# Perceiver kernel, expert phase of layer 0: token weights by small TensorE products of transposed key factors, kept in DRAM; expert products in split rounded form

## Chip, cores and metric

One core of one Trainium2 chip runs the whole program. The metric is the device time of one execution in microseconds (us); the time of a version is the median over its runs. Lower is better.

## What is computed

A two-layer model on 1024 tokens (32 x 32) of width 512. Layer 0 is cross attention, gated attention with an MLP, and a feed-forward block with a routed part; layer 1 is cross attention over 257 context rows, a scan and a last MLP. The change lies in the feed-forward block of layer 0:

```
q = (x @ Wq) per head h of 4;  sim = q @ keys          # 64 first keys x, 64 second keys y
top 8 of each, all 8 x 8 sums, top 8 of those           # expert number x * 64 + y, 2048 experts
w = silu(x @ down_embed[idx]) * softmax(scores)
experts = sum over heads and 8 choices of w * up_embed[idx]
mlp = silu(x @ Wg + bg) * (x @ Wu + bu) @ Wd + bd
return mlp + experts
```

The kernel does not gather experts. For every token it makes a dense row of 2048 token weights (the softmax weight of each chosen expert, zero elsewhere, summed over the four heads), and computes silu(down @ y) times the token weights, times up. Weights of choices with a first key of 32 or more all go to the last expert.

## The kernel before

Every engine has its own program, and semaphores tie them. Stages end with a drain of all engines. Tokens are columns; C2 = 2 chunks c of 512 tokens, TT = 8 tiles t of 128 tokens, o numbers blocks of 128 outputs, and the hidden width of 2048 is done in NQ = 4 quarters j of 512. PSUM has eight banks of 128x512: four (`open_act`) are emptied by ACT, four (`open_dve`) by DVE, each in the order in which TensorE opens them.

Products of the MLP are in *split rounded form* (`split_linear`, L739): each fp32 operand is the sum of a rounded part (fp32r, "high") and a rest ("low"), and high\*high + low\*high + high\*low takes 12 matmuls of 128x512 for one unit of 512 inputs, 128 outputs, 512 tokens. ACT makes the high parts, DVE the low parts, of the weights too (`piece_high`, `piece_low`, eight pieces ahead). Products in plain fp32 (`linear`, L498) take 4 matmuls a unit.

Stage C, in the order of its steps:
- Layer norm, queries (`cq`), similarities (`sim`, L787), and the split of the normed input y (`y_high`, `y_low`).
- Gated MLP. For each quarter j: eight pairs of units `cg` (gate, emptied by ACT with Silu, L1418) and `cu` (up, emptied by DVE, L2046), then eight units `cd` (`down`, L749), which wait for the low part of the hidden tile (`hidden_low`, L2035, waited for at L751). Between these, DVE routes the token tiles, two per quarter, piece by piece, in the list `ROUTE` (L1998): `route_keys` (top 8), `route_pairs`, `route_chosen`, `route_counts` (how many second keys go with each first key), `route_ranks` (the rank of each second key, L1973), `route_factors`.
- Expert phase. 32 steps n = (quarter j, tile t). `factors_in` and `factors_out` are the expert products in plain fp32 on y and on the weighted hidden tile. The token weights of a step: `products` on ACT makes 32 copies of 64 columns, each scaled by one factor (L1397); `spread` on DVE (L2004 to L2024) compares 2048 elements, multiplies, adds the heads; `factor_rows` (L820) transposes on TensorE; `weigh` (L2026) multiplies into the hidden tile.

Small products on parts of the array stand in other stages: `scores` (L664, 32x32 tiles) and `values` (L678, four tiles on the diagonal) in the attention of stage B, `weighted` (L953, four column tiles) in stage D.

Stage D begins with layer norm and `memory(0, ...)` (L857), products of context and the weights `wmh`, `wml`.

SP issues all DMAs in one written order; `load(i)` brings one weight block of 1 MB and first waits until its slot's last user is done.

```
STEPS, LEAD, LAG = TT * NQ, 3, 5
...
v.tensor_tensor(tmp, RC["Tx"][:, t, :, xs].unsqueeze(3).to_broadcast([128, PH, 8, 64]),
                RC["Ry"][:, t].unsqueeze(2).to_broadcast([128, PH, 8, 64]), ALU.is_gt)
```

Of the kernel before, what the change touches and what calls it, by code (L numbers as in the profile page):

```python
# [35 lines left out]
def constant_tables():  # L36
# [24 lines left out]
    tabs["rank"] = np.tile(np.arange(8.0) - 8.0, (128, 1))  # L61
# [34 lines left out]
def perceiver(nc, dram, out):  # L96
# [6 lines left out]
    with ctx:  # L103
# [56 lines left out]
        with ExitStack() as until_last:  # L160
# [5 lines left out]
            wmh = shared_r("wmh", [128, 2, 4, 512])  # L166
# [3 lines left out]
            wml = shared_r("wml", [128, 2, 4, 512])  # L170
# [28 lines left out]
        with ExitStack() as until_last:  # L199
# [4 lines left out]
            rank_eq, count_eq = small_ints("rank_eq", [128, 256, 8]), small_ints("count_eq", [128, 128, 8])  # L204
            iota8, rank8 = small_ints("iota8", [128, 64, 8]), small_ints("rank8", [128, 1, 8])
            keys8, counts8 = small_ints("keys8", [128, 2 * PH, 8]), small_ints("counts8", [128, PH, 8])
        rank_eq, count_eq, iota8, rank8, keys8, counts8 = (x[:, :, :] for x in (rank_eq, count_eq, iota8, rank8, keys8, counts8))
# [5 lines left out]
        def region(spec, base=R, limit=RN):  # L213
# [18 lines left out]
        slot_full = [sem(f"slot_full{i}") for i in range(6)]  # L232
        spilled = [sem(f"spilled{i}") for i in range(2)]
# [17 lines left out]
            "a_khi", "a_qhi", "a_whi", "a_wlo", "a_chi", "a_clo", "a_bhi", "a_blo", "a_ahi", "a_ctx", "c_topin", "c_topexp", "c_p", "c_kb", "c_fac", "c_ee", "c_mul", "c_y", "c_wq",  # L251
# [69 lines left out]
        expert_slots = iter([(turn[0] + i) % 2 for i in range(2)] + [2, 3, 4, 5] + [(turn[0] + i) % 2 for i in range(2)])  # L321
        for j in range(-1, NQ + 1):
            if j + 1 < NQ:
                plan(("ce", j + 1), rows4("downT", 0, 512 * j + 512), next(expert_slots))
            if j >= 1:
                plan(("cf", j - 1), rows4("L0_ffn_up_embed", 512 * j - 512), next(expert_slots))
        D_FIRST = len(loads)
        for h in range(2):
            plan(("dm", h), rows4("L1_xattn_Wm", 0, 512 * h), 4 + h)
# [23 lines left out]
        def first_high_of(i):  # L353
# [6 lines left out]
        RC = region([("sim", (8, 512)), ("kb", (4, 128)), ("Tx", (8, PH, 32)), ("Ex", (8, PH, 32)), ("Ry", (8, PH, 64)),  # L360
                     ("Ey", (8, PH, 64)), ("eq", (1, 2048)), ("s", (4, 512)), ("xv", (1, 8)),
                     ("pj", (2, 512)), ("tv", (8, 8)), ("ti", (8, 8)), ("cand", (PH, 64)), ("rep", (PH, 64)),
                     ("t8", (PH, 8)), ("na", (PH, 8)), ("z", (1, 4)), ("rz", (1, 4)), ("ge", (PH, 8)), ("rs", (PH, 8)),
                     ("sd", (8, 64)), ("sel", (PH, 64))])
# [3 lines left out]
        SJ = [H[:, 0], H[:, 1], XN]  # L368
# [14 lines left out]
        EE = [RC["sim"][:, 0:4].rearrange("p t n -> p (t n)"), RC["sim"][:, 4:8].rearrange("p t n -> p (t n)"),  # L383
              RC["s"].rearrange("p t n -> p (t n)")]
        ct = H[:, 0, 0:2, :].rearrange("p k (b m) -> p (k b m)", b=2).rearrange("p (k b m) -> p k b m", k=4, b=2)
        ct_first = arena[:, 3, :, :].rearrange("p k (b m) -> p k b m", b=2)
# [58 lines left out]
        def b1_order(j):  # L445

            return [(o, c) for c in range(C2) for o in range(4)] if j == 0 else [(o, c) for o in range(4) for c in range(C2)]
# [14 lines left out]
        def _(pe):  # L462
# [286 lines left out]
            def down(name, j, ready, first):  # L749
                for c in range(C2):  # L750
                    pe.wait_ge(ready, first + 8 * j + (4 * c + 4 if (name, j) == ("b2", 0) else 7 + c))  # L751
                    for o in range(4):
                        b = open_dve((name, j, c, o))
                        split_linear(b, (name, j), o, hid_high, hid_low, c).then_inc(dve_bank_full, 1)
                        if c == C2 - 1:
                            piece_used[piece_no[((name, j), o)]] = (dve_bank_full, UV.n)


            for j in range(NQ):
                for o, c in b1_order(j):  # L760
# [14 lines left out]
            pe.wait_ge(S["c_wq"], 16)  # L775
            for c in range(C2):
                features(2, c)
                normed(pe, 2, c)
# [27 lines left out]
            def factors_in(n):  # L806
                j, t = n // TT, n % TT
                if t == 0:
                    weight(("ce", j))
# [347 lines left out]
        def _(act):  # L1157
# [286 lines left out]
            for t in range(4):  # L1444
                hidden(0, t)
# [1138 lines left out]
```

## Time and profile before

| | |
|---|---|
| median of 3 runs | 2295.05 us (2292.68 to 2303.32) |
| the profiled execution | 2294.39 us, its span 2292.6 us |
| mean granted TensorE clock | 0.971 |
| busy in the span | PE 2114.7, DVE 1280.5, ACT 917.4, POOL 94.8 us |
| first gated-MLP matmul of stage C | starts at 720.3 us |
| first expert matmul | starts at 988.9 us |
| last expert matmul | ends at 1256.1 us |

The profiled execution's own time is 1.8 us more than its span. "Busy" of TensorE counts overlapped matmuls once; a matmul of 128x512 in fp32r shows 389 ns but the next begins 227 ns after it. "Granted clock" is TensorE's clock as a share of 2.4 GHz; a half is the level of 1.2 GHz. A name like L746 is a line of the kernel before.

### The profile page before, as it was taken

Reading aid. Unit: us, or ns where it says so; the run is one execution under the profiler, and the core shown is the slowest. Engines: PE = TensorE matmul, PEld = TensorE weight load, DVE = VectorE, ACT = ScalarE, POOL = GpSimd, SP = SyncE. Lnnn points to the kernel's source line nnn. Section 1 sums busy time; section 2 is a strip of 40 time slices with the busy share of each in tenths; the row PEclk is TensorE's granted clock in tenths of the full one; section 3 lists DMA queues with packets and bytes.
Section 4 is the critical chain, followed back from the end, with each engine's and each line's share of the span. In section 5 each row is a group of like instructions: output and inputs, shape, how many; then the busy total and the mean of one; then the engine's idle time right before and its main releaser. Section 6 shows DMA issues by size and latency. Waiting matters only on the chain. (4 is left out here: it accounts for less than half of the span.)

```text
span 2292.6 us, 35473 instructions
## 1 busy us (share of the span) xinstructions
PE 2114.7 (92%) x14758; PEld 1530.3 (67%) x14758; DVE 1280.5 (56%) x2082; ACT 917.4 (40%) x2208; POOL 94.8 (4%) x119
## 2 busy tenths in 40 slices
PE   6989888689999999989998999999999999988899
PEld 5763444368876888844445788777878778774587
DVE  4246388463343887799998310445344443536563
ACT  3224333142334333489997332322232322313342
POOL 0000001000000000100000000100000000000122
PEclk9999899789999999999999999999999999999999
DMA  6120000111210101120002144412121121232000
GB/s 236 42 77 0 1 2 2 39 37 56 72 44 1 56 19 56 56 92 1 19 0 94 36 142 133 134 43 84 42 84 43 52 74 42 66 111 90 1 1 37
DMA packets 84871, 127.06 MB, mean 55 GB/s; under 512 B 6998, under 2 KB 48470, under 8 KB 84248
## 3 DMA queue, kind: packets, MB, share of 16 engines
q1 hardware_dynamic: 84712, 124.79, 16.4%
q8 instruction: 118, 1.93, 0.4%
q14 instruction: 41, 0.34, 0.1%
HBM read 109.83 MB, written 14.94 MB: 54 GB/s over the span
## 5 line engine op out<-in xcount | busy, mean ns | idle before, releaser
L1167 ACT ACTIVATE R<-bank 128x512 f32<-128x512 f32 (+3 forms) x157 | 93.0, 598 | 460.9 <-PE bank L866 332.3
L1397 ACT ACTIVATE R<-R 128x64 f32<-128x64 f32 x1024 | 248.3, 366 | 0.0
L866 PE MATMUL bank<-cth,wmh 128*128 128x512 f32 x512 | 209.6, 409 | 12.4 <-ACT arena L1494 6.3
L866 PE MATMUL bank<-cth,wml 128*128 128x512 f32 x512 | 203.7, 398 | 0.0
L866 PE MATMUL bank<-ctl,wmh 128*128 128x512 f32 x512 | 203.5, 397 | 0.0
L501 PE MATMUL bank<-XN,arena 128*128 128x512 f32 x320 | 144.9, 606 | 0.4 <-ACT R L1328 0.4
L866 PEld LDWEIGHTS bank<-cth,wmh 128*128 128x128 f32 x512 | 97.2, 190 | 41.9 <-issue 22.3
L501 PE MATMUL bank<-Y,arena 128*128 128x512 f32 x256 | 117.3, 604 | 0.0
L2119 DVE COPY Y<-bank 128x512 f32<-128x512 f32 x128 | 79.2, 682 | 59.3 <-PE bank L904 59.3
L866 PEld LDWEIGHTS bank<-cth,wml 128*128 128x128 f32 x512 | 97.1, 190 | 22.6
L501 PEld LDWEIGHTS bank<-XN,arena 128*128 128x128 f32 x320 | 60.9, 195 | 75.5 <-issue 73.4
L866 PEld LDWEIGHTS bank<-ctl,wmh 128*128 128x128 f32 x512 | 97.3, 190 | 20.4
L746 PE MATMUL bank<-hid_high,piece_high 128*128 128x512 f32 x256 | 100.0, 391 | 6.2 <-DVE hid_low L2037 6.2
L1494 ACT ACTIVATE arena<-bank,small 128x289 f32<-128x289 f32 x128 | 62.6, 503 | 100.3 <-PE bank L915 53.5
L746 PE MATMUL bank<-y_high,piece_high 128*128 128x512 f32 x256 | 99.7, 389 | 0.0
L746 PE MATMUL bank<-hid_low,piece_high 128*128 128x512 f32 x256 | 99.6, 389 | 0.0
L746 PE MATMUL bank<-hid_high,piece_low 128*128 128x512 f32 x256 | 99.6, 389 | 0.0
L746 PE MATMUL bank<-y_high,piece_low 128*128 128x512 f32 x256 | 99.6, 389 | 0.0
L746 PE MATMUL bank<-y_low,piece_high 128*128 128x512 f32 x256 | 99.6, 389 | 0.0
L2106 DVE TENSOR_TENSOR ctl<-H,cth 128x2048 fp32r<-128x2048 f32 x15 | 34.4, 2292 | 103.4 <-ACT cth L1469 103.4
L1205 ACT ACTIVATE piece_high<-arena 128x512 fp32r<-128x512 f32 x80 | 48.8, 624 | 104.5 <-PE bank L746 103.4
L501 PEld LDWEIGHTS bank<-Y,arena 128*128 128x128 f32 x256 | 49.5, 195 | 60.1 <-issue 59.8
(412 smaller groups left out, 4464.7 us busy)
## 6 DMA issues: line engine op xcount, KB each, us to landing
H<-in_ctxT SPq DMA_DIRECT2D x30, 512.0 KB, 5.1
arena<-in_L_attn_mlp_w SPq DMA_DIRECT2D x8, 1024.0 KB, 5.4
arena<-spill SPq DMA_DIRECT2D x32, 256.0 KB, 5.5
spill<-R SPq DMA_DIRECT2D x3, 2048.0 KB, 8.3
spill<-XN SPq DMA_DIRECT2D x3, 2048.0 KB, 8.3
arena<-in_L_ffn_Wg SPq DMA_DIRECT2D x4, 1024.0 KB, 6.8
arena<-in_L_ffn_Wu SPq DMA_DIRECT2D x4, 1024.0 KB, 5.2
arena<-in_L_ffn_Wd SPq DMA_DIRECT2D x4, 1024.0 KB, 5.4
```

What stands on the lines that cost most here:

```text
L501: last = mm(bank, w[:, k, cols_], x[:, k, xc], start=(k == 0), stop=(k == 3 and not more))
L746: last = mm(b[:, :], w_, x_[:, k, ch(c)], start=(k == 0 and i == 0), stop=(k == 3 and i == 2))
L866: last = mm(b[:, :].rearrange("p (a c) -> p a c", a=2), w_, c_[:, k, :, :], start=(k == 0 and n_ == 0), stop=(k == 3 and n_ == 2))
L1167: fn(dst, src, ACT.Copy).then_inc(act_bank_free, 1)
L1205: fn(piece_high[:, n % PIECES], W(name)[:, :, tl(o)], ACT.Copy).then_inc(S["w_high"], 1)
L1397: last = fn(EE[n % 3][:, a:a + 64], RC["Ey"][:, t, h, :], ACT.Copy, scale=RC["Ex"][:, t, h, 8 * j + x:8 * j + x + 1])
L1494: fn(RDa["p"][:, g, 320 * (bb % 2):320 * (bb % 2) + 289], b[:, 0:289], ACT.Exp, bias=small[:, 16 + x:17 + x], scale=HD1 ** -0.5, accum_out ...
L2106: v.tensor_tensor(ctl[:, :, :, :], ct if pr else ct_first, cth[:, :, :, :].bitcast(f32), ALU.subtract).then_inc(S["d_clo"], 1)
L2119: v.tensor_copy(RD["vt"][:, 2 * (bb % 2) + blk, 512 * half:512 * half + 512], b[:, :]).then_inc(dve_bank_free, 1)
```

## The change

The 32 steps of the expert phase are gone, with `products`, `spread`, `factor_rows`, `weigh` and `route_ranks`, and the addition on POOL that put y together again.

Token weights are now made in the gated MLP, one token tile at a time. For each head and rank b of a second key, `route_first_keys` makes 32 numbers over the first keys, `route_second_keys` makes a 0/1 row over the 64 second keys, and DVE transposes both in 32x32 blocks, so that (head, b) lies on 32 partitions. `expert_sums(t, half)` then makes, for each of 64 tokens of a half, two products of 32 rows by 64 by 16 on TensorE, 128 in all, and two more for the last expert; ACT empties the banks (`sums_of`), SP stores a tile of 1 MB to DRAM and later reads it back in 256 KB blocks.

The expert phase is then like the MLP: `ce` and `cf` are units of 12 matmuls in split rounded form; DVE multiplies the token weights in. The order of queries and similarities changes, the first tile is routed before the MLP, and the first weights and contexts of stage D are loaded and split earlier.

TensorE, from the diff:

```diff
+                        elif o in half_after:
+                            expert_sums(2 * j + 1, half_after.index(o))
+
+            def expert_sums(t, half):
+
+                pe.wait_ge(S["c_pairs"], t + 1)
+                two = {i: open_act(("w", t, i)) for i in (2 * half, 2 * half + 1)}
+                for r in range(32):
+                    for par in range(2):
+                        for i, b in two.items():
+                            heads = slice(32 * i, 32 * i + 32)
+                            mm(b[64 * par:64 * par + 64, 16 * r:16 * r + 16], RC["yT"][heads, :, r], RC["xT"][heads, par:32:2, r],
+                               start=(r == 0), stop=False, tile_position=(32 * i, 64 * par), skip_group_check=True)
+                for i, b in two.items():
+                    mm(b[:, :].rearrange("p (r m) -> p m r", m=16)[:, 15, :], RC["xv"][:, 0, :], tab("ident")[:, 32 * i:32 * i + 32],
+                       start=False, stop=True, skip_group_check=True).then_inc(act_bank_full, 1)
 
...
-            pe.wait_ge(S["x_low"], 2 * C2)
+            similarities(1)
             for j in range(NQ):
                 for o in range(4):
                     for c in range(C2):
+                        if j == 0 and o == 0:
+                            pe.wait_ge(S["x_low"], C2 + c + 1)
                         b = open_act(("cg", j, o, c))
                         split_linear(b, ("cg", j), o, y_high, y_low, c).then_inc(act_bank_full, 1)
                         b = open_dve(("cu", j, o, c))
                         split_linear(b, ("cu", j), o, y_high, y_low, c).then_inc(dve_bank_full, 1)
-                    piece_used[piece_no[(("cg", j), o)]] = (act_bank_full, UA.n)
+                        if 2 * o + c in (1, 2):
+                            expert_sums(2 * j, 2 * o + c - 1)
+                    piece_used[piece_no[(("cg", j), o)]] = (act_bank_full, UA.at[("cg", j, o, C2 - 1)] + 1)
                     piece_used[piece_no[(("cu", j), o)]] = (dve_bank_full, UV.n)
-                down("cd", j, S["h_low"], 32)
...
-            def factor_rows(n):
-                j, t = n // TT, n % TT
-                pe.wait_ge(S["c_p"], n + 1)
-                b = open_dve(("pt", j, t))
-                for e in range(4):
-                    last = nc.tensor.transpose(b[:, tl(e)], RC["pj"][:, t % 2, tl(e)], tab("ident"))
-                last.then_inc(dve_bank_full, 1)
...
+                down("cd", j, S["h_low"], 32, (1, 2))
+
+            for j in range(NQ):
+                for o, c in up_order(j):
+                    b = open_act(("ce", j, o, c))
+                    split_linear(b, ("ce", j), o, y_high, y_low, c).then_inc(act_bank_full, 1)
+                    if c == C2 - 1:
+                        piece_used[piece_no[(("ce", j), o)]] = (act_bank_full, UA.n)
+                down("cf", j, S["h_low"], 64)
```

ACT and DVE:

```diff
+            def sums_of(t, half):
+
+                if t and half == 0:
+                    act.wait_ge(sums_out, 16 * t)
+                for i in (2 * half, 2 * half + 1):
+                    copy_out(RC["sums"][:, :, 32 * i:32 * i + 32], unit(("w", t, i))[:, :].rearrange("p (r m) -> p m r", m=16))
...
+            for j in range(NQ):
+                for i, (o, c) in enumerate(up_order(j)):
+                    u = 8 * j + i
+                    activated(("ce", j, o, c), 32 + u)
+                    if i:
+                        act.wait_ge(S["c_scaled"], u)
+                        hidden_high(32 + u - 1, *up_order(j)[i - 1])
+                    if c == C2 - 1:
+                        split_high(piece_no[(("ce", j), o)] + PIECES)
+                act.wait_ge(S["c_scaled"], 8 * j + 8)
+                hidden_high(32 + 8 * j + 7, *up_order(j)[7])
...
-                on_act(("ce", j, 3 if t < 4 else 7))
-                b = unit(("pt", j, t))
-                x = SJ[j % 3][:, :, tl(t)]
-                v.tensor_tensor(x, b[:, :].rearrange("p (e n) -> p e n", e=4), x, ALU.mult).then_inc(dve_bank_free, 1)
-
-            def hidden_low(u):
-                j, o, c = u // 8, u // 2 % 4, u % 2
+                v.tensor_reduce(RC["xv"][:, 0, 127:128], RT["rs"].rearrange("p h a -> p (h a)"), AX.X, ALU.add)
+                step(v.tensor_tensor(RC["Ex"], RT["sd"][:, 0, 0:128].rearrange("p (h x) -> p h x", h=PH), rz.to_broadcast([128, PH, 32]),
+                                     ALU.mult))
+
+            first_keys = RC["xf"].rearrange("p (h b) x -> p h b x", h=PH)
+
+            def route_first_keys(t):
+
+                for b in range(8):
+                    last = v.scalar_tensor_tensor(first_keys[:, :, b, :], RC["Tx"], float(b), RC["Ex"], ALU.is_gt, ALU.mult)
+                step(last)
+                step(v.tensor_tensor(RC["xf"], RC["xf"], RT["sd"][:, 0, 128:160].unsqueeze(2).to_broadcast([128, 32, 32]), ALU.mult))
+                v.transpose(RC["xT"], RC["xf"].rearrange("p n x -> p x n"))
+
+            def route_second_keys(t):
+
+                step(v.tensor_tensor(RC["yf"], iota8.unsqueeze(1).to_broadcast([128, PH, 64, 8]),
+                                     keys8[:, 4:8, :].unsqueeze(2).to_broadcast([128, PH, 64, 8]), ALU.is_equal))
+                v.transpose(RC["yT"].rearrange("p y (h b) -> p y h b", h=PH), RC["yf"].rearrange("p h y b -> p y h b")
+                            ).then_inc(S["c_pairs"], 1)
+
+            ROUTE = [route_keys, route_pairs, route_chosen, route_counts, route_factors, route_first_keys, route_second_keys]
+            DOWN_PIECES = {(0, 0): 1, (0, 1): 2, (0, 2): 3, (0, 3): 4, (1, 0): 5, (1, 1): 6}
+
```

SP:

```diff
+            sums = dram["sums"]
+
+            def store_sums(t):
+                sp.wait_ge(act_bank_free, UA.at[("w", t, 3)] + 1)
+                sp.dma_start(sums[:, :, tl(t)].rearrange("m p n -> p m n"), RC["sums"]).then_inc(sums_out, 16)
+
+            def load_sums_of(u):
+                j, (o, c) = u // 8, up_order(u // 8)[u % 8]
+                if u >= 8:
+                    sp.wait_ge(S["c_scaled"], u - 7)
+                else:
+                    sp.wait_ge(S["c_pairs"], u + 1)
+                sp.wait_ge(sums_out, 16 * (4 * c + 4))
+                sp.dma_start(RC["sim"][:, u % 8, :], sums[4 * j + o, :, ch(c)]).then_inc(sums_in[u % 8], 16)
+
+            load(first_split + 2)
...
+                store_sums(2 * j)
+                load(first_split + 3 * j + 4)
+                store_sums(2 * j + 1)
+                load(first_split + 3 * j + 5)
+                if j < NQ - 1:
+                    load(first_split + 3 * j + 6)
+            for u in range(4):
+                load_sums_of(u)
+            load(first_split + 15)
+            for u in range(4, 8):
+                load_sums_of(u)
+            for h in range(2):
+                sp.dma_start(dm_raw[:, h], rows4("L1_xattn_Wm", 0, 512 * h)).then_inc(S["d_dm"], 16)
+            for u in range(8, 32):
+                load_sums_of(u)
+                if u in (15, 23):
+                    load(first_split + 16 + (u // 8 - 1) * 2)
+                    load(first_split + 17 + (u // 8 - 1) * 2)
 
             two = dram["ctxT"].rearrange("(k p) (b m) -> p k b m", p=128, m=M)
 
```

On TensorE in the first quarter of the gated MLP, as it stands now (L764 and L767 are `expert_sums`, L742 is `split_linear`; R holds the transposed factors), rows just ahead of the first half of tile 0's small products and behind it:

```order
L742 MATMUL bank<-y_high,piece_high 128x512
L742 MATMUL bank<-y_low,piece_high 128x512
L742 MATMUL bank<-y_high,piece_low 128x512
L764 MATMUL bank<-R 64x16 x128
L767 MATMUL bank<-consts,R 128x32 x2
L742 MATMUL bank<-y_high,piece_high 128x512
L742 MATMUL bank<-y_low,piece_high 128x512
```

Such a group of 130 stands at 16 places of the gated MLP, four in each quarter; before, there was none, and L746 followed on L746.

On DVE before, at the fifth and the sixth pair of units of the first quarter (L1976 and L1978 are `route_ranks`, L1960 to L1996 `route_factors`):

```order
L2037 TENSOR_TENSOR hid_low<-R,hid_high 128x512
L1976 TENSOR_TENSOR rank_eq<-iota,keys 128x2048
L1978 TENSOR_TENSOR rank_eq<-rank_eq,rank 128x2048
L2046 SCALAR_TENSOR_TENSOR R<-bank,cols,R 128x512
L2037 TENSOR_TENSOR hid_low<-R,hid_high 128x512
L1960 TENSOR_TENSOR rank_eq<-rank_eq 128x256x4
L1960 TENSOR_TENSOR rank_eq<-rank_eq 128x256x2
L1983 TENSOR_TENSOR R<-rank_eq 128x256
```

On DVE now, ahead of the first `cu` unit (L2005), the end of tile 0's routing (L1969 to L1972 are `route_first_keys`, L1976 and L1978 `route_second_keys`):

```order
L1961 TENSOR_TENSOR R<-R 128x128
L1969 SCALAR_TENSOR_TENSOR R<-R 128x4x32 x8
L1971 TENSOR_TENSOR R<-R 128x1024
L1972 STREAM_TRANSPOSE R<-R 128x1024
L1976 TENSOR_TENSOR R<-iota,keys 128x2048
L1978 STREAM_TRANSPOSE R<-R 128x2048
L2005 SCALAR_TENSOR_TENSOR R<-bank,cols,R 128x512
L1898 MAX R<-R 128x8 x8
```

The rank products of the list are gone; the two new pieces stand behind the sixth and the seventh `cu` unit of each quarter, and for tile 0 ahead of the first.

## Rows read from the trace of the kernel before

**Rows 1.** Windows: us, busy (x instructions) of PE, PEld, DVE, ACT, POOL; clock, DMA, GB/s.
```profile
720.00:785.00 65.00, 63.46 (x282) 52.30 (x282) 47.02 (x145) 23.33 (x36) 0.00 (x0) 1.00 0.05 17
1030.00:1230.00 200.00, 185.92 (x495) 82.80 (x495) 189.89 (x155) 200.00 (x815) 0.00 (x0) 1.00 0.07 24
```

**Rows 2.** Timeline of PE: start, us, what [idle before]; 38 matmuls lie from 980.03 to 988.64.
```profile
966.98 0.50 PE L746 MATMUL bank<-hid_high,piece_high 128*128 128x512 f32 x1 [1.54 <-DVE hid_low L2037]
...
980.03 0.39 PE L746 MATMUL bank<-hid_high,piece_high 128*128 128x512 f32 x1
988.64 0.39 PE L746 MATMUL bank<-hid_high,piece_low 128*128 128x512 f32 x1
988.87 13.89 PE L501 MATMUL bank<-Y,arena 128*128 128x512 f32 x32
...
1245.13 10.96 PE L501 MATMUL bank<-H,arena 128*128 128x128 f32 x96
```

**Rows 3.** Groups of small and large products: xcount, busy, mean ns, idle before.
```profile
L664 PE MATMUL bank<-H 32*32 32x32 f32 x1024 | 11.7, 214 | 8.4 <-issue 8.4
L678 PE MATMUL bank<-R 32*32 32x33 f32 x1024 | 15.9, 237 | 24.1 <-DVE R L1831 15.1 <-issue 8.9
L953 PE MATMUL bank<-Y,R 128*32 128x64 f32 x2048 | 35.4, 221 | 2.5 <-DVE XN L2181 1.5 <-issue 1.1
L664 PEld LDWEIGHTS bank<-H 32*32 32x32 f32 x1024 | 10.8, 112 | 9.9 <-issue 9.1 <-DVE H L1851 0.2
L746 PEld LDWEIGHTS bank<-y_high,piece_high 128*128 128x128 f32 x256 | 48.1, 188 | 9.9
```

**Rows 4.** Timeline of PE, one set of 256 small products, and what follows.
```profile
268.27 1.74 PE L664 MATMUL bank<-H 32*32 32x32 f32 x161
272.31 1.14 PE L664 MATMUL bank<-H 32*32 32x32 f32 x95 [2.30 <-issue]
273.87 6.43 PE L501 MATMUL bank<-XN,arena 128*128 128x512 f32 x8 [0.42 <-ACT R L1328]
```

**Rows 5.** Groups of DVE in the gated MLP; last, two of other stages.
```profile
L2046 DVE SCALAR_TENSOR_TENSOR R<-bank,cols,R 128x512 f32<-128x512 f32 x32 | 24.0, 750 | 37.2 <-PE bank L746 37.2
L2037 DVE TENSOR_TENSOR hid_low<-R,hid_high 128x512 fp32r<-128x512 f32 x32 | 21.8, 682 | 0.4
L1927 DVE MAX8 R<-R 128x8 f32<-128x64 f32 x64 | 8.8, 210 | 0.0
L1983 DVE TENSOR_TENSOR R<-rank_eq 128x256 f32<-128x256 bf16 x8 | 4.9, 617 | 0.3
L1985 DVE TENSOR_TENSOR R<-R 128x256 f32<-128x256 f32 x8 | 3.3, 418 | 0.0
L1996 DVE TENSOR_TENSOR R<-R 128x128 f32<-128x128 f32 x7 | 2.0, 284 | 0.0
L1769 DVE STREAM_TRANSPOSE R<-R 128x1024 f32<-128x1024 f32 x1 | 1.2, 1245 | 6.6 <-DMA R<-scratch 6.6
1239.31 2.29 DVE L2015 TENSOR_TENSOR R<-R 128x2048 f32<-128x2048 f32 x1
```

**Rows 6.** Timeline of ACT ahead of the gated MLP.
```profile
720.58 0.60 ACT L1167 ACTIVATE R<-bank 128x512 f32<-128x512 f32 x1 [0.30 <-PE bank L787]
721.19 1.28 ACT L1418 ACT_TABLE_LOAD   x1
```

**Rows 7.** Timeline of PE, after longer idle times.
```profile
1012.91 0.83 PE L820 MATMUL bank<-consts,R 128*128 128x128 f32 x4 [2.41 <-DVE R L2021]
1013.54 5.16 PE L501 MATMUL bank<-Y,arena 128*128 128x512 f32 x8
...
1273.69 0.77 PE L866 MATMUL bank<-cth,wmh 128*128 128x512 f32 x1 [3.16 <-DVE R L1671]
```

**Rows 8.** Page, DMA issues: out<-in xcount, KB each, us to landing.
```profile
arena<-spill SPq DMA_DIRECT2D x32, 256.0 KB, 5.5
spill<-R SPq DMA_DIRECT2D x3, 2048.0 KB, 8.3
```

More of the change, by code:

```diff
@@ L232, in perceiver @@
         slot_full = [sem(f"slot_full{i}") for i in range(6)]
+        sums_in = [sem(f"sums_in{i}") for i in range(8)]
+        sums_out = sem("sums_out")
         spilled = [sem(f"spilled{i}") for i in range(2)]
@@ L775, in _, with similarities @@
             pe.wait_ge(S["c_wq"], 16)
+            def similarities(c):
+                on_act(("cq", 3, c))
+                pe.wait_ge(S["c_kb"], 16)
+                for t in range(4 * c, 4 * c + 4):
+                    b = open_act(("sim", t))
+                    for j in range(4):
+                        last = mm(b[:, tl(j)], H[:, 0, j, tl(t)], RC["kb"][:, j, :], start=True, stop=True)
+                    last.then_inc(act_bank_full, 1)
             for c in range(C2):
                 features(2, c)
+                if c:
+                    similarities(0)
                 normed(pe, 2, c)
@@ L1033, in _ @@
                 released[(w, half)] = (S["d_plo"], 4 * (g_ + 1))
-            for h in range(2):
-                released[("dm", h)] = (stage_done, 4 * (stage[0] + 1))
             end_stage()
@@ L1371, in _, with similarities @@
             end_stage()
+            def similarities(c):
+                for t in range(4 * c, 4 * c + 4):
+                    copy_out(RC["sim"][:, t, :], unit(("sim", t))[:, :])
             warm()
@@ L1433, in _ @@
+                sums_of(2 * j + 1, 0)
+                sums_of(2 * j + 1, 1)
                 for o in range(4):
                     split_high(piece_no[(("cd", j), o)] + PIECES)
-            def hidden(j, t):
-                b = unit(("ce", j, t))
-                fn(SJ[j % 3][:, t % 4, ch(t // 4)], b[:, :], ACT.Silu).then_inc(act_bank_free, 1)
-            products(1)
-            act.wait_ge(S["h_low"], 32 + 8 * NQ)
-            products(2)
-            act.wait_ge(dve_bank_full, UV.at[("cd", 3, C2 - 1, 3)] + 1)
@@ new lines, in _ @@
+            inputs_low(0)
+            inputs_low(1)
+            for piece in ROUTE[4:]:
+                piece(0)
+            for j in range(NQ):
+                for i in range(8):
+                    o, c, u = i // 2, i % 2, 8 * j + i
+                    on_act(("cg", j, o, c))
+                    b = unit(("cu", j, o, c))
+                    v.scalar_tensor_tensor(RC["s"][:, u % 4, :], b[:, :], col("L0_ffn_bu", 4 * j + o), RC["s"][:, u % 4, :],
+                                           ALU.add, ALU.mult).then_inc(dve_bank_free, 1)
+                    if i:
+                        hidden_low(u - 1, (i - 1) // 2, (i - 1) % 2)
+                    if i < 7:
+                        ROUTE[i](2 * j + 1)
+                    elif j < NQ - 1:
+                        route_keys(2 * j + 2)
+                    if c == C2 - 1 and o < 3:
```

375 lines of the change are left out of this document (121 added, 254 removed).

## The prediction

> **What bounds the kernel now.** I read the windows first, then TensorE's timeline, then the groups of instructions. In the gated MLP TensorE is busy 63.46 of 65 us, ACT 23.33 and DVE 47.02 at the full clock, so this stretch costs what its matmuls cost [rows 1]. In the expert phase ACT is busy all of 200 us, DVE 189.89 and TensorE 185.92 [rows 1]: three engines are near full, and ACT, with the scaled copies of `products`, has no gap at all. The timeline gives the two prices of a large product [rows 2]. In split form 38 steps take from 980.03 to 988.64 us, 0.227 us each, so a unit of 12 costs 2.72 us. The plain fp32 ones (32 in 13.89 us) cost 0.434 us, 1.74 us a unit. The split form is dearer for TensorE; what it buys is an expert phase in which nothing else is needed. The phase lasts from 988.9 to 1256.1 us, 267.2 us [rows 2].
>
> **What goes.** All 267.2 us. With them go 1024 copies on ACT, the comparing and adding on DVE and 128 transposes; they lie beside each other within that time, so they aren't counted again.
>
> **Expert products.** 4 quarters x 16 units x 2.72 us = 174.1 us on TensorE. Beside it a unit of `ce` asks of DVE a scaling, a low part and a weight's low part, at 0.68 us each [rows 5]: 2.0 us of 2.72. ACT has three passes of about 0.6 us [rows 6]. So TensorE bounds it. At the turn to `cf` it waits: before, the turn in the MLP cost 1.54 us for a product on DVE and a low part [rows 2]; now the last unit passes Silu, the scaling and the low part of the one before, some 0.69 + 0.68 + 0.68 and hops, 2.25 us. The first quarter walks its chunks so that it needs no wait, so 3 x 2.25 = 6.8 us. Together 180.9 us.
>
> **Small products.** 2048 of 32 rows by 64 weight columns by 16 columns, none like them in the trace. Three groups are near [rows 3]: 32x32x32 in sixteen tiles, busy 11.7 us for 1024, 11 ns each; 32x32x33 on four tiles in turn, 15.5 ns; 128x32x64 on four column tiles, 17.3 ns. Ours alternate among four tiles. A weight load takes 112 ns for 32 columns and 188 for 128 [rows 3], 0.8 ns a column, so ours carries more load and less product. Lower bound: 11 ns. Upper bound: a load of 64 columns that nothing hides, 64 x 0.8 = 51 ns plus a part of the product, 55 ns. I take 17 ns, by the two groups on four tiles. A group of 130 is then 2.2 us, 0.24 for the two full-height products and 0.2 for the change of tiling (estimates), 2.6 us; sixteen make **42 us**. The fetch gap of 2.30 us came after 161 products in a row [rows 4]; a group of 130 between large products should stay below it, so I charge none.
>
> A rule speaks against this price. The rows hold products of 32 columns at 11 ns. The Trainium skill, "TensorEngine Tiling (Array Packing)", section Performance Considerations, says that each matmul carries some 60 cycles of overhead, whatever its few columns: 25 ns at 2.4 GHz. By it 2048 would cost 51 us, and the sum would come out 16 us higher, at no change; the rows are faster than the rule, and they decide.
>
> **DVE's list.** Ranks go (two passes over 2048 bf16, then sums); in come eight products over 128 numbers, one over 1024, a transpose of 1024, a comparison of 2048 into fp32 and a transpose of 2048. A pass over 64 numbers is issued every 0.14 us, one over 128 lasts 0.28 [rows 5], so eight take about 1.6; 1024 take 1.2 (0.28 for 128, 2.29 for 2048). The transpose of 1024 took 1.245 us with neighbours in a row, but now reads numbers 128 bytes apart. A sum that reads every 16 bytes took 617 ns for 256 results, an ordinary one 418 [rows 5]; with that ratio, 1.9. So `route_first_keys` costs 4.7 us, `route_second_keys` 2.3 + 2.4 = 4.7. They stand behind the sixth and seventh `cu`. There DVE has the scaling, a low part, the piece and two weights' low parts, 0.75 + 0.68 + 4.7 + 1.37 = 7.5, and then 0.75 + 0.68 + 4.7 = 6.1 us, against 2 x 5.44 of TensorE: it is 2.7 us behind when the last `cu` is done, and `cd` waits for `hidden_low` behind that. Four quarters: **10.8 us** over the 1.54 that each turn has now. In the `cd` stretch DVE needs about 28 us for TensorE's 21.8 and two groups; it makes that up before the next sums are asked for, nothing charged. Bounds for this term: 0 if passes overlap more, 20 if both transposes are read at the strided price.
>
> **The first tile.** It must be routed before the second `cu`. Its first four pieces lie under the query products. `route_factors` needs ACT's exponentials, which come after the last similarity copies (ending 721.2 [rows 6], about 1 us later with the new order) and a table load of 1.28 us: 724.2. Then DVE has the rest of `route_factors` (nine small passes of 0.19 to 0.42 us, 2.3 in all) and the two new pieces, 2.3 + 4.7 + 4.7 us, to 736. TensorE, started at 720.3 as now (similarities and queries are only exchanged), gets there at 731.2. **4.8 us**, once.
>
> **The clock.** After an idle 2.41 us the next eight plain matmuls took 5.16 us in place of 3.60; after 3.16 us a split one shows 0.77 where 0.39 is usual [rows 7, 2]: the level of 1.2 GHz for some 3.5 us. After 1.54 us nearly nothing is lost [rows 2]. The change makes five waits of 4 us and more, at 2.1 us lost each, and three of 2.25, at 1.2: **14 us**; bounds 0 and 20.
>
> **At nothing.** ACT's 32 emptyings of token weights (0.6 us each, 19 us) lie in an MLP where it is a third busy [rows 1]; uncovered, a bank would come free late. SP's eight stores of 1 MB and 32 loads of 256 KB: 2 MB took 8.3 us to land and 256 KB 5.5 [rows 8]. A store is due a whole half quarter before its buffer is wanted; the loads of the second chunk need tile 7, stored some 20 us before. Each waits in SP's one queue behind weight loads that come two blocks early; if a load were late, Silu's buffer would hold TensorE after eight units, 21.8 us. POOL's addition was under TensorE. In stage D one wait (context split) goes and one (`memory_low`, 2.3 us behind the other low part) comes in its place; +-2.
>
> **Sum.** -267.2 + 180.9 + 42 + 4.8 + 10.8 + 14 = -14.7 us. Against the profiled execution (2294.4; span 2292.6 and 1.8 around it) that is 2279.7. The median shown is 0.7 above this execution, which I leave. **Forecast 2280 us.** Break-even is at a small product of 24 ns.
>
> **Rivals.**
> 1. *Weight loads aren't hidden (slower).* Place: each of the 16 groups. Two of every four small products load the same 32 partitions, and each load is as wide as two of the loads in the rows; columns lie 128 bytes apart, moving ones 256. On DVE such reading cost 1.5 times [rows 5]; nothing in the trace shows it for TensorE. For: 51 ns by slope. Against: 128x32 loads follow at 17.3 ns though 27 ns wide by the same slope, so they overlap. At 45 ns a product: 28 x 2048 = +57 us, **2337 us**. It decides from 24 ns on. The rule that points here is the Trainium skill's "SBUF — State Buffer", on 16-byte cachelines: full bandwidth wants two hits in a line. DVE's rows agree with it.
> 2. *Everything overlaps.* 11 ns a product, no clock lost: -13 - 14, **2253 us**. For: the sixteen-tile group. Against: fewer tiles here.
> 3. *The clock falls after each group.* After a set of 256 with its gap, eight plain matmuls took 6.43 us in place of 3.60 [rows 4]. Sixteen times 2.8: +45, **2325 us**. Against: the 128x32 products are spread over a stretch at full clock.
> 4. *Token weights come late from DRAM*, so that what went from ACT returns as a wait: one load time and a half at the start of the phase, +8, **2288 us**.
>
> **Chances.** Forecast 0.45 (its own range 2265 to 2296), rival 1 0.25, rival 2 0.15, rival 3 0.08, rival 4 0.07. A measurement of this kernel tells about 0.5%, 11.5 us, from no change. Faster by more: most of the forecast (0.29), rival 2 and a little of 4: 0.46. Slower by more: rivals 1 and 3 and a tail of the forecast: 0.36. Within: 0.18. The range of 8 in 10 reaches from rival 2 to the middle of rival 1: 2252 to 2338.
>
> **What would show it.** L764 in groups of 128 lasting 2.2 us: right; 5 us or more: rival 1. Large matmuls at 0.227 us right behind a group: rival 3 wrong. From the first `ce` to the last `cf` 181 us plus the clock's share; waits for `hidden_low` of 4.2 us four times, for `c_pairs` once. I am wrong if `ce` waits for the loads of sums, or if DVE comes so late that groups wait in every quarter.

## The result, and the profile after

The changed kernel takes 2426.8 us (median of 4 runs, 2419.0 to 2427.88) against 2295.39 us before (4 runs): 1.0566 times, 95% interval 1.0545 to 1.0588. The forecast was 2280 us with a range up to 2338, so the time lies outside the range and on the other side. The profiled execution has a span of 2425.1 us against 2292.6 of before, 132.5 us more.

The page's slices first. This is the granted clock in 40 equal slices, before and then now. In the second half it was near full before; now it sags over eight slices in a row, the gated MLP:

```profile
PEclk9999899789999999999999999999999999999999
PEclk9999888899998887878799999999999999999999
```

The groups of instructions for the small products, TensorE's matmuls and weight loads (PEld):

```profile
L764 PE MATMUL bank<-R 32*64 32x16 f32 x4096 | 139.0, 284 | 4.0 <-DVE R L1978 4.0
L764 PEld LDWEIGHTS bank<-R 32*64 32x64 f32 x4096 | 137.3, 224 | 10.0 <-issue 5.6 <-DVE R L1978 4.4
L767 PE MATMUL bank<-consts,R 128*128 128x32 f32 x64 | 17.0, 406 | 0.0
```

The program issues 2048 small products; the trace has 4096 records at L764. So **a float32 product is two records**, and all that I had priced by a row of the trace before was priced by the record. Busy 139.0 us over 4096 is 33.9 ns a record, 68 ns a product, where I had put 17.

The timeline of TensorE, the first two groups with what follows them (start, us, what, idle before):

```profile
737.18 8.62 PE L764 MATMUL bank<-R 32*64 32x16 f32 x256 [3.95 <-DVE R L1978]
745.73 1.06 PE L767 MATMUL bank<-consts,R 128*128 128x32 f32 x4
746.61 0.78 PE L742 MATMUL bank<-y_high,piece_high 128*128 128x512 f32 x1
747.18 0.63 PE L742 MATMUL bank<-y_low,piece_high 128*128 128x512 f32 x1
747.61 0.63 PE L742 MATMUL bank<-y_high,piece_low 128*128 128x512 f32 x1
...
753.76 8.65 PE L764 MATMUL bank<-R 32*64 32x16 f32 x256
762.34 1.06 PE L767 MATMUL bank<-consts,R 128*128 128x32 f32 x4
...
796.29 0.50 PE L742 MATMUL bank<-hid_high,piece_high 128*128 128x512 f32 x1 [3.88 <-DVE hid_low L1991]
```

A group lasts 8.6 us where I had 2.2, and seven or eight large matmuls behind it start 0.43 us apart in place of 0.227. Windows of the first group, then of the second group and of what follows it (length, busy with instructions of PE, PEld, DVE, ACT and POOL, then the clock):

```profile
737.20:741.00 3.80, 3.80 (x118) 3.80 (x119) 3.73 (x26) 0.64 (x1) 0.00 (x0) 0.50 0.00 0
741.00:745.70 4.70, 4.70 (x146) 4.70 (x144) 2.76 (x16) 0.00 (x0) 0.00 (x0) 0.50 0.03 7
753.80:758.00 4.20, 4.20 (x131) 4.20 (x132) 2.83 (x8) 0.00 (x0) 0.00 (x0) 0.84 0.02 4
758.00:762.30 4.30, 4.30 (x134) 4.30 (x132) 0.00 (x0) 0.00 (x0) 0.00 (x0) 0.50 0.01 4
762.50:764.50 2.00, 2.00 (x7) 1.81 (x8) 0.00 (x0) 1.08 (x2) 0.00 (x0) 0.50 0.00 0
```

Two things are to be seen. The clock falls from 2.4 to 1.2 GHz inside the second group, although TensorE has no gap, and stays low behind it; the first group, behind a wait of 3.95 us, runs at 1.2 GHz from its start. And the small products don't care: 256 records take 8.62 us in the first group and 8.65 in the second, of which a part ran at full clock, 33.7 and 33.8 ns each. What limits them isn't TensorE's clock.

The parts of the change, against the forecast's sum:

| part | forecast, us | measured, us | from |
|---|---|---|---|
| old expert phase gone | -267.2 | -267.2 | [rows 2] |
| expert products with their waits | 180.9 | 182.8 | timeline, 1201.86 to 1384.7 |
| small products, L764 and L767 | 42 | 156 | groups, 139.0 + 17.0 |
| first tile | 4.8 | 4.0 | timeline, 3.95 |
| four turns to `cd` | 10.8 | 9.3 | 4 waits of 3.88 for 1.54 |
| clock, large matmuls of the gated MLP | 14 | 42 | rest, below |
| before and behind (start of MLP, stage D) | 0 | 5.6 | 1.7 + 3.9 |
| sum | -14.7 | 132.5 | |

The gated MLP lasts from 722.0 to 1201.86 us, 479.9. Its large matmuls took 262.4 before (268.6 less four waits of 1.54). With 156 for the groups and 19.5 for five waits, 42 are left: what the large matmuls took longer at the lower clock. The forecast's 14 also held 3.6 for the turns of the expert phase; what these lost is in the 182.8. Of the 147 us between forecast and measurement 114 lie in the small products and 28 in the clock.

The 5.6 us before and behind can't be put down to the change: over the eleven profiled kernels with the new expert phase, this one and those of the experiments, the stretch ahead of the gated MLP takes 717.2 to 723.1 us and the one behind the expert phase 1036.7 to 1041.9, though the edits leave nearly all of the work there as it is.

### The profile page after: what moved, and what is told of

Same layout as the page of the kernel before. It is cut to its first block and busy times, and to the rows that moved or that the text cites. A ratio compares the mean times of both kernels' runs of the same rounds, so it can differ in the third digit from the quotient of the medians.

```text
span 2425.1 us, 43019 instructions
## 1 busy us (share of the span) xinstructions
PE 2252.5 (93%) x18950; PEld 1744.1 (72%) x18950; DVE 1153.6 (48%) x2066; ACT 725.1 (30%) x1279; POOL 83.7 (3%) x111
## 5 line engine op out<-in xcount | busy, mean ns | idle before, releaser
L1139 ACT ACTIVATE R<-bank 128x512 f32<-128x512 f32 x189 | 110.5, 597 | 632.0 <-PE bank L839 329.3
L742 PE MATMUL bank<-hid_high,piece_high 128*128 128x512 f32 x384 | 162.7, 424 | 21.6 <-DVE hid_low L1991 21.6
L742 PE MATMUL bank<-hid_low,piece_high 128*128 128x512 f32 x384 | 160.0, 417 | 0.0
L742 PE MATMUL bank<-hid_high,piece_low 128*128 128x512 f32 x384 | 159.0, 414 | 0.0
L742 PE MATMUL bank<-y_high,piece_high 128*128 128x512 f32 x384 | 158.2, 412 | 0.4 <-DVE y_low L1986 0.4
L742 PE MATMUL bank<-y_low,piece_high 128*128 128x512 f32 x384 | 156.2, 407 | 0.0
L742 PE MATMUL bank<-y_high,piece_low 128*128 128x512 f32 x384 | 155.5, 405 | 0.0
L764 PEld LDWEIGHTS bank<-R 32*64 32x64 f32 x4096 | 137.3, 224 | 10.0 <-issue 5.6
L764 PE MATMUL bank<-R 32*64 32x16 f32 x4096 | 139.0, 284 | 4.0 <-DVE R L1978 4.0
L839 PEld LDWEIGHTS bank<-cth,wmh 128*128 128x128 f32 x512 | 97.2, 190 | 42.0 <-issue 19.5
L742 PEld LDWEIGHTS bank<-hid_high,piece_high 128*128 128x128 f32 x384 | 79.3, 207 | 41.3 <-DVE hid_low L1991 24.5
```

The source lines that it names most:

```text
L742: last = mm(b[:, :], w_, x_[:, k, ch(c)], start=(k == 0 and i == 0), stop=(k == 3 and i == 2))
L764: mm(b[64 * par:64 * par + 64, 16 * r:16 * r + 16], RC["yT"][heads, :, r], RC["xT"][heads, par:32:2, r], start=(r == 0), stop=False, tile_ ...
L839: last = mm(b[:, :].rearrange("p (a c) -> p a c", a=2), w_, c_[:, k, :, :], start=(k == 0 and n_ == 0), stop=(k == 3 and n_ == 2))
L1139: fn(dst, src, ACT.Copy).then_inc(act_bank_free, 1)
```

## The experiments

Each edit is made to the changed kernel (2426.8 us) and timed beside the kernel before. Medians are given, and a ratio is to the kernel before, which came to 2293.6 to 2296.1 us beside them. Times without a ratio are of a single execution. Where a length of the gated MLP is given, it is read from the profiled executions (479.9 us in the change).

**Without the small products.**

```diff
-                for r in range(32):
+                for r in range(0):
...
-                       start=False, stop=True, skip_group_check=True).then_inc(act_bank_full, 1)
+                       start=True, stop=True, skip_group_check=True).then_inc(act_bank_full, 1)
```

The last pair lets the product of L767 open its bank, since nothing is written there before it.

> The changed kernel without the 2048 small products (32 rows by 64 by 16); the two full-height products of each group, the copies, the stores and loads and all of DVE's list stay. The token weights are therefore zero apart from the last expert's. Theory A (the groups of small products and the clock behind them are the whole loss): the gated MLP falls from 479.9 to about 268.6 + 13 of waits + 17 for the full-height products and their slow neighbours, some 300 us, and the time is near 2427 - 180 = 2247 us, below the kernel before. Rival B (DVE's longer list, the DRAM round trip or the new expert phase share the loss): above 2290 us.

2248.24 us, ratio 0.979 (0.9767 to 0.9812). All the rest of the change is a gain of 46 us. The gated MLP falls from 479.9 to 301.5 us, so the whole difference lies there. The groups cost 178.6 us: 139.0 at L764, 8.0 at L767 (17.0 before the edit, 9.0 now, mean 264 ns in place of 406), and 31.6, the rest, in the large matmuls behind them. That is the price of a small product, the place of rival 1, and rival 3 together.

**The layout.** Three kernels read the same number of bytes from other places, so that the token weights are wrong: neighbouring words on both sides, on the weight side alone, and on the moving side alone.

```diff
-  RC["yT"][heads, :, r]
+  RC["yT"].rearrange("p y t -> p (y t)")[heads, 64 * r:64 * r + 64]
-  RC["xT"][heads, par:32:2, r]
+  RC["xT"].rearrange("p x t -> p (x t)")[heads, 32 * r + 16 * par:32 * r + 16 * par + 16]
```

> The changed kernel, but the small products read 64 and 16 adjacent numbers of the same two tiles, in place of columns 128 and 256 bytes apart (the token weights are wrong numbers for that). Theory S (reading with a stride sets the 33.7 ns per record): 17 ns or less per record, a group under 5 us, time about 2427 - 16 x 4.3 = 2358 us or lower. Rival L (a load of 64 columns that nothing hides): unchanged, 33 ns and 2427 us. Rival C (the low clock sets it): unchanged too.

> Only the weight side (64 columns) reads adjacent numbers. If the stride counts and the load is the longer part: nearly all of the gain of the run with both sides packed. If the stride of the moving side counts: little.

> Only the moving side (16 columns) reads adjacent numbers. If the load of weights sets the pace: within 10 us of the changed kernel's 2427 us, 33 ns a record.

2363.45, 2364.09 and 2416.21 us; the gated MLP is 58, 56 and 11 us shorter. The first is 5 us above what was expected of it, the last just past the 10 us that it was given. The groups of each, in this order:

```profile
L764 PE MATMUL bank<-R 32*64 32x16 f32 x4096 | 75.1, 215 | 17.4 <-issue 13.5 <-DVE R L1978 4.0
```

```profile
L764 PE MATMUL bank<-R 32*64 32x16 f32 x4096 | 76.8, 217 | 16.7 <-issue 12.8 <-DVE R L1978 4.0
```

```profile
L764 PE MATMUL bank<-R 32*64 32x16 f32 x4096 | 125.5, 270 | 4.0 <-DVE R L1978 4.0
```

The weight side alone, whose columns lie 128 bytes apart in the change, takes 62 us off the busy time and both sides 64; the moving side alone takes off 13.5, and 2 beside a packed weight side. Packed, a record comes to about 16 ns at full clock: in the timeline of the first of these kernels 227 of them take 3.55 us, 15.6 ns, and behind them comes an idle time that nothing in the trace releases. The first group, at 1.2 GHz from its start to its end, needs 7.03 us for its 256, 27.5 ns each, so a packed record does depend on the clock:

```profile
732.34 7.03 PE L764 MATMUL bank<-R 32*64 32x16 f32 x256 [3.97 <-DVE R L1978]
747.79 3.55 PE L764 MATMUL bank<-R 32*64 32x16 f32 x227
752.35 1.04 PE L764 MATMUL bank<-R 32*64 32x16 f32 x29 [1.00 <-issue]
...
900.87 3.92 PE L764 MATMUL bank<-R 32*64 32x16 f32 x256
```

It looks like the gap of [rows 4], which I had ruled out for groups of 130; with two records a product the groups are of 256. It gives back 13 of the 62 to 64 us. In the changed kernel, at 34 ns a record, it doesn't show, so it didn't cost anything there.

**Packed, with the right numbers.** VectorE's transpose writes token by token, so its writes are strided in TensorE's place.

```diff
-  v.transpose(RC["yT"].rearrange("p y (h b) -> p y h b", h=PH),
+  v.transpose(RC["yT"].rearrange("p y t -> p (y t)").rearrange("p (t y) -> p t y", t=32)
+              .rearrange("p (h b) y -> p y h b", h=PH),
...
-  RC["yT"][heads, :, r]
+  RC["yT"].rearrange("p y t -> p (y t)").rearrange("p (t y) -> p t y", t=32)[heads, r, :]
```

> The changed kernel with its results kept: VectorE's transpose writes yT token by token, so that the weight side of each small product reads consecutive words; VectorE's writes are strided in its place. Theory A (the 128-byte stride of the weight side's columns doubles a record, and it is free to move that stride to VectorE's write): groups go from 8.6 to about 4.6 us, as in the run that misread the packed layout, L1978's transpose stays within 1 us of its 2.31, and the time comes near 2364 to 2370. Theory B (the stride costs wherever it is): the transpose on VectorE goes to 4 us or more, route_second_keys becomes a wait of PE at the groups, and the time stays above 2390.

2379.03 us, ratio 1.036 (1.033 to 1.0389), between the two theories, 9 us from A and 11 from B. The groups fall as in the runs before, but the transpose pays:

```profile
L764 PE MATMUL bank<-R 32*64 32x16 f32 x4096 | 77.9, 218 | 19.0 <-issue 13.6 <-DVE R L1978 5.3
L1978 DVE STREAM_TRANSPOSE R<-R 128x2048 f32<-128x2048 f32 x8 | 29.8, 3719 | 0.3
```

3.72 us in place of 2.31, eight times, and TensorE's waits for `hid_low` come to 26.4 us (21.6 before the edit), 5.1 the longest; the wait ahead of the first group is 5.3 for 4.0. The layout of the weight side alone gained 63 us in its one execution; with the stride moved to VectorE's write 48 are left. Of the 15 between them 9 are in the gated MLP of the profiled executions, 6 of these in the two waits named.

**Half of the products.** Every second `r` is left out, so half of the token weights are missing.

```diff
-                for r in range(32):
+                for r in range(0, 32, 2):
```

> The changed kernel with every second small product of a group left out (1024 of 2048; half the token weights are missing). Theory A (a record has a fixed 34 ns, and the clock falls inside a group after some us): groups of 4.3 us, 16 x 4.3 = 69 us less, and the slow matmuls behind each group go if the clock falls only in a longer stretch (some 43 us more less), which gives 2315 to 2358. Theory B (the clock falls at any group): groups of 4.3 us and granted clock at 0.50 behind them still, 2350 to 2358.

2362.76 us, 5 us above theory B; the gated MLP is 64.5 us shorter. The windows of its second group:

```profile
750.00:752.00 2.00, 2.00 (x61) 1.96 (x60) 1.75 (x4) 0.00 (x0) 0.00 (x0) 1.00 0.00 0
752.00:754.60 2.60, 2.60 (x78) 2.57 (x75) 1.08 (x5) 0.00 (x0) 0.00 (x0) 0.87 0.02 6
754.60:757.00 2.40, 2.40 (x8) 2.11 (x9) 0.00 (x0) 1.08 (x2) 0.00 (x0) 0.50 0.00 0
```

The busy time of L764 is 71.9 us for 2048 records, 35.1 ns each for 33.9: nearly the same price per record. The clock falls behind a group of 4.56 us as behind one of 8.6, and it did so at all sixteen, so halving the group gave 67 us of busy time and no clock. In the packed kernels above even groups of 3.92 us lost it.

**VectorE's list.** The pieces of the odd tiles move one slot ahead from `route_counts` on, so that the last slot of a turn is empty.

```diff
...
+  SLOTS = [[route_keys], [route_pairs], [route_chosen, route_counts], [route_factors],
+           [route_first_keys], [route_second_keys], []]
...
-                        ROUTE[i](2 * j + 1)
+                        for piece in SLOTS[i]:
+                            piece(2 * j + 1)
```

> The changed kernel with VectorE's routing pieces of the odd tiles in other slots of a turn (one piece earlier, the last slot empty), nothing else. Theory A (PE waits 3.9 us at each of the four turns from cu to cd because VectorE is behind with a routing piece in the last slot): those four waits go from 3.9 to about 1.5 us, as before the change, and the time falls by 7 to 11 us, to about 2417. Theory B (the wait there is a chain of ScalarE and VectorE on the last hidden unit): no change of the waits, and the time stays within 3 us.

2399.81 us, 27 less than the change (1.0456, 1.0429 to 1.0483, against 1.0566). The waits fell as theory A said, from 3.88 to 1.51 us, 9.5 in all with those of the expert phase (21.6 to 12.1), but the gain is more than that. The windows of the wait and of what follows it, first in the changed kernel, then here:

```profile
792.30:796.30 4.00, 0.12 (x2) 0.01 (x1) 3.97 (x6) 0.63 (x2) 0.00 (x0) 1.00 0.00 0
796.30:800.00 3.70, 3.70 (x11) 3.00 (x12) 3.63 (x26) 2.33 (x4) 0.00 (x0) 0.67 0.01 2
```

```profile
789.80:791.30 1.50, 0.04 (x1) 0.04 (x1) 1.44 (x4) 0.66 (x2) 0.00 (x0) 1.00 0.00 0
791.30:794.00 2.70, 2.70 (x12) 2.20 (x13) 2.63 (x25) 2.30 (x3) 0.00 (x0) 1.00 0.00 0
```

The wait of 3.9 us costs the clock behind it as well; the one of 1.5 doesn't. How much that is, the next run tells with no group in the way: both edits together, no small products and the earlier slots.

> The changed kernel with VectorE's pieces in the earlier slots and without the 2048 small products (token weights are missing; the correction column of each bank is still written). Theory A (the earlier slots are worth some 20 us also where no group slows the clock, since the four waits of 3.9 us lost 2.4 us and the clock behind each): 2228 to 2238. Theory B (most of the 27 us that the earlier slots gave came through the groups): 2240 or more.

2227.0 us (ratio 0.969, 0.9667 to 0.9713), 21.2 below the run without products in the old order: 9.5 of waits and the rest at the clock (in the gated MLP and the expert phase, 256 matmuls each of `hid_high`, `hid_low` and `piece_low` at a mean of 404, 397 and 397 ns, for 419, 410 and 409: 10 us). Theory A holds. The other 6 of the 27 us are no more than the scatter: the runs of the two kernels with groups spread over 9 and 14 us, and their profiled executions are 16 us apart, 17 of them in the gated MLP (479.9 and 462.7).

**Products in bfloat16.** Both factors are stored in bfloat16, packed token by token: the counts are exact in it, the first factor is rounded to it, and so the token weights are.

```diff
+  xT_r = factor_part("xT_r", [128, 32, 32])
+  yT_r = factor_part("yT_r", [128, 32, 64])
...
-  v.transpose(RC["xT"], RC["xf"].rearrange("p n x -> p x n"))
+  v.transpose(xT_r, xf_r.rearrange("p n x -> p x n"))
...
-  v.transpose(RC["yT"].rearrange("p y (h b) -> p y h b", h=PH), RC["yf"].rearrange("p h y b -> p y h b")
+  v.transpose(yT_r.rearrange("p (h b) y -> p y h b", h=PH), yf_r.rearrange("p h y b -> p y h b")
...
-  RC["yT"][heads, :, r], RC["xT"][heads, par:32:2, r]
+  yT_r[heads, r, :], xT_r[heads, par:32:2, r]
```

> The changed kernel with both factors of the small products stored in bfloat16 (the counts 0 and 1 are exact in it, the first factor is rounded, so the token weights lose digits) and the weight side packed token by token. Theory A (a record costs some 16 ns packed, and a product is one record in bfloat16 instead of two in float32): 2048 records, groups of 2.0 to 2.3 us, little or no clock lost behind them, and a time of 2280 to 2300. Theory B (a product costs its own time, in whatever number of records): groups of 4.6 us as with packed float32, and about 2360.

2296.59 us, where the two kernels meet. The groups:

```profile
L778 PE MATMUL bank<-xT_r,yT_r 32*64 32x16 bf16 x2048 | 20.2, 185 | 9.7 <-DVE yT_r L1992 9.7
L1992 DVE STREAM_TRANSPOSE yT_r<-yf_r 128x2048 bf16<-128x2048 bf16 x8 | 75.4, 9423 | 0.3
L1986 DVE STREAM_TRANSPOSE xT_r<-xf_r 128x1024 bf16<-128x1024 bf16 x8 | 15.4, 1927 | 0.3
```

Half the records, and 20.2 us for them. The timeline and the windows of the second group:

```profile
749.09 1.22 PE L778 MATMUL bank<-xT_r,yT_r 32*64 32x16 bf16 x128
```

```profile
749.00:751.00 2.00, 2.00 (x134) 1.86 (x134) 1.70 (x4) 0.31 (x1) 0.00 (x0) 1.00 0.04 8
751.00:754.00 3.00, 3.00 (x14) 2.44 (x13) 1.14 (x5) 1.02 (x3) 0.00 (x0) 1.00 0.41 118
```

A group of 1.22 us leaves the clock at full speed; only the first group, behind its wait of 9.7 us, runs at 1.2 GHz. These groups are shorter and of another type at once, so which of the two keeps the clock isn't shown. But VectorE's strided bfloat16 transpose takes 9.42 us, which I hadn't foreseen, and the waits for `hid_low` rise from 21.6 to 44.1 us, and the one ahead of the first group from 4.0 to 9.7: 28 us of TensorE's time.

**A version meant to beat both.** VectorE transposes in float32 as in the change; ScalarE, a third busy there, copies both factors to bfloat16, the second one packed; VectorE's pieces stand in the earlier slots. As in the run before, the first factor is rounded to bfloat16.

```diff
+            def halved(t):
+                act.wait_ge(S["c_pairs"], t + 1)
+                fn(xb[:, :, :], RC["xT"], ACT.Copy)
+                fn(yb[:, :, :], RC["yT"].rearrange("p y t -> p t y"), ACT.Copy).then_inc(S["c_halved"], 1)
...
-                pe.wait_ge(S["c_pairs"], t + 1)
+                pe.wait_ge(S["c_halved"], t + 1)
...
-  RC["yT"][heads, :, r], RC["xT"][heads, par:32:2, r]
+  yb[heads, r, :], xb[heads, par:32:2, r]
```

> A version meant to beat both. As the changed kernel, with VectorE's routing pieces in the earlier slots, VectorE's transposes in float32 as in the changed kernel, and ScalarE copying both factors of a tile to bfloat16, the second one packed token by token, for the small products to read. Theory A (what costs is the number of records, the weight side's stride and the clock that long groups lose; VectorE's bfloat16 transpose of 9.4 us was a side cost of that edit alone): groups of 1.2 to 2 us, waits for hid_low at the turns near 1.5 us, no clock lost, and a time of 2255 to 2275. Theory B (ScalarE's copies of some 4 us a tile delay its hidden halves and PE waits at the turns instead): waits of 3 us or more at the four turns, and a time near 2290.

2258.87 us (2251.5 to 2259.45, 5 runs), ratio 0.982 (0.9797 to 0.9843): faster than the change by 168 us and than the kernel before by 1.8%. Groups of TensorE and ScalarE, and TensorE's longest waits:

```profile
L769 PE MATMUL bank<-xb,yb 32*64 32x16 bf16 x2048 | 20.6, 185 | 9.7 <-ACT yb L1378 8.6 <-issue 1.0
L772 PE MATMUL bank<-consts,R 128*128 128x32 f32 x64 | 10.5, 289 | 0.0
L1378 ACT ACTIVATE yb<-R 128x2048 bf16<-128x2048 f32 x8 | 31.9, 3994 | 0.0
L1377 ACT ACTIVATE xb<-R 128x1024 bf16<-128x1024 f32 x8 | 8.4, 1050 | 10.5 <-DVE R L1992 10.4
```

```profile
PE bank L747 <- DVE hid_low L2006: 12.1, 7, 2.0
PE bank L769 <- ACT yb L1378: 8.6, 1, 8.6
```

Except for 1.3 us at a large matmul, ScalarE's 5.0 us a tile are hidden but for the first tile, whose wait grows from 4.0 to 8.6 us. The granted clock is 0.98 over 722 to 1130 us; in the change it is 0.80 over 722 to 1202. The price of the products is now 31.9 us (2258.87 - 2227.0), for 178.6: 20.6 at L769, 1.6 more at L772 than its 8.9 without products, 4.6 of the longer wait, the 1.3, 1.0 of idle time at L769 that nothing in the trace releases, and 3 that stay open.

## Why the prediction was wrong

**The small products, the step that failed.** "2048 of 32 rows by 64 weight columns ... I take 17 ns" had three errors.
First, the rows were read by the record: a float32 matmul is two. L664's 1024 records are 512 products, and the range of 11 to 17 ns was one of 22 to 35 a product. This was to be seen before: the loop of the program says how many products there are. With 34 ns a product the term would have been some 35 us larger and the forecast 2315.
Second, the stride. Packed, a record costs 15.6 ns at full clock and 18.3 on average, at the upper end of [rows 3]; in the change it costs 33.9. Rival 1 had its place and its sign right, and the 128 bytes. Its price was reasoned from the load's width, 51 ns, though; the same width packed costs half. PEld is busy for 137.3 of the 139.0 us, and packing the loads' side takes off 62 us where the other side alone takes off 13.5: the loads set most of the pace. The Trainium skill, "SBUF — State Buffer", section Specifications (TRN2), says that full bandwidth wants two hits in a 16-byte line; the runs agree in direction, on the weight side (62 us), and less on the moving side, where columns lie 256 bytes apart and packing them gives 13.5. The Trainium skill, "TensorEngine Tiling (Array Packing)", section Performance Considerations, gives 60 cycles of overhead a matmul, by an estimate 25 ns at 2.4 GHz. As a floor the trace doesn't bear it out: in bfloat16 128 products took 1.22 us, 9.5 ns each. But I had set that rule aside because the rows were faster, at 11 ns; by the product they were at 23 to 35, so that reason was wrong, and so was my price below it.
Third, the upper bound. 55 ns a product was below the measured 68, so that even the range was too narrow. The 0.2 us that the term held for the change of tiling no run shows: the second group starts 0.31 us after the last large matmul, where these follow each other 0.23 apart, so 0.1 is seen there and not 0.2.

**The plain form's price.** The same reading spoiled "1.74 us a unit": 32 records in 13.89 us are 16 products, 3.47 us for a unit of four. The split form, 2.72 us, is the cheaper one for TensorE, not the dearer. Nothing in the sum hung on it, since the old phase was taken by its length.

**Full-height products.** Forecast 0.24 us a group, 3.8 in all; measured 17.0. They too are two records each, which alone makes 7.6 of my 3.8; without the groups they took 9.0, and behind the groups, at the low clock, 17.0.

**The clock.** Rival 3, with 0.08, came true beside it: 31.6 us against its 45. I had argued that the 128x32 products were spread over a stretch at full clock; a group between large matmuls at full activity looked harmless. It isn't: float32 groups of 3.92 to 8.8 us lose the clock, bfloat16 ones of 1.22 don't. The rivals were priced apart; in fact a dearer product makes a longer group and that takes the clock too, so their prices add up: 68 ns a product is 104 us over the term, and with rival 3's 45 the sum would have come to 2429 us, near the 2426.8.

**Expert products.** 180.9 forecast, and 3.6 for the clock behind the turns in another term; 182.8 measured with both. The three turns wait 2.0 us each for my 2.25. Right.

**VectorE's list.** The turn was put at 2.7 us more, measured 2.34 (3.88 less 1.54); `route_first_keys` was 4.7 and is about 5.0, with the strided transpose at 2.10 for my 1.9; `route_second_keys` 4.7 and 4.6. Right, and the earlier slots undo it.

**First tile, clock after waits.** 4.8 forecast, 3.95 measured. For the clock after the five long waits I had 2.1 us each; the run without products gives about 10.5 us for all five (a gated MLP of 301.5 us, less the 268.6 of before, 9.0 at L767, 4.0 for the first tile and 9.3 at the turns). For these five the forecast had 10.5 as well.

**Costs put at nothing.** ScalarE's emptyings, SP's stores and loads showed no wait: no `ce` waits for sums, `c_pairs` is waited for once. Rival 4 is refuted. In stage D the wait for `wml` that I had named is there, 2.7 us; TensorE stood idle for 2.5 us at the same place before, so the one wait did pay for the other. The 3.9 us that the rest of the kernel took more are within the spread named above.

**The gap of [rows 4].** I ruled it out by the length of a group. It doesn't show in the change, but only because products were slow; the packed runs have it, 12.8 to 13.6 us. What it waits for no run shows.

## What to carry to other kernels

Before a row's mean is used as a price, compare its count with the loop that issues it: here a float32 product was two records, and every price by the row was half. Price a small product by the layout it reads as well as by its shape, the weight side first, and try what moving the stride to another engine costs there: ScalarE had room for it, VectorE did not. And price a group by what stands behind it: long runs of narrow float32 products took the clock from the large matmuls that followed, a fifth of what the groups cost, and bfloat16 groups of 1.2 us left it alone.

## What the runs showed of the hardware

- Small float32 products whose weight columns lie 128 bytes apart took 33.7 to 33.9 ns a record, two records a product; packed 15.6 ns at full clock; bfloat16 packed 9.5 (128 in 1.22 us), one record a product. Bfloat16 with the columns apart wasn't tried, so what the type and the layout each give there stays open.
- The strided record takes the same time whether a group runs wholly at 1.2 GHz or partly at 2.4 (33.7 and 33.8 ns). The packed ones don't: float32 27.5 ns at a clock of 0.50 and 15.6 at full, bfloat16 14.7 (128 in 1.88 us) and 9.5.
- The clock fell within float32 groups of narrow products, or right behind them, without a gap in them, at all sixteen places; groups of 1.22 us in bfloat16 kept it. What in these groups makes it fall, the runs don't tell apart.
- VectorE's transpose of 128x2048: 2.31 us in float32, 3.72 with strided float32 writes, 9.42 with strided bfloat16 writes. The transpose of 128x1024 took 2.10 us in float32 and 1.93 in bfloat16, so the type alone doesn't slow it there; what makes the 9.42 the runs don't tell.
